# Last self attention: where ScalarE copies the turned weights, between the logarithms of the distances or ahead of them

## The chip, the cores and the metric

The kernel runs on one core of one Trainium2 chip. The metric is device microseconds from start to end of one execution; the kernel before takes 5246.27 us, the median of three runs (5241.81 to 5249.77).

## The reference

The whole is a four-layer stack on x of shape 128 x 32 x 128 (batch, positions, width), each layer a cross attention, a self attention and a feed-forward part with residuals. The change touches the self attention of the last layer alone (16 heads of 8, 32 positions per batch entry), cut here to what it computes:

```python
x = x + _L3_attn_ref(_layernorm(x), Wq, Wk, Wv, Wo)

def _L3_attn_ref(x, Wq, Wk, Wv, Wo):
    q, k, v = (split_heads(x @ W.T) for W in (Wq, Wk, Wv))
    diff_sq = jnp.maximum(q_norm_sq + k_norm_sq - 2.0 * qk, 0.0)
    denom = jnp.maximum((1.0 - q_norm_sq) * (1.0 - k_norm_sq), 1e-06)
    cosh_arg = jnp.maximum(1.0 + 2.0 * diff_sq / denom, 1.0)
    distance = jnp.where(cosh_arg > 1.0, jnp.arccosh(...), 0.0)
    attn = jax.nn.softmax(-distance, axis=-1)
    return (attn @ v, heads joined) @ Wo.T
```

## The kernel before

The 4096 rows of x lie in SBUF as 32 tiles of 128 rows, four batch entries each (TILES = 32, NB = 4). A part of the stack walks over the tiles as a software pipeline. `Plan.run` (L317) unrolls some rounds at either end and puts two rounds into each pass of a hardware loop (step 2) for the rest. In round t an engine works on several tiles at once: `r.third` the layer norm's statistics of t+3, `r.after` the projections of t+2, `r.coming` the scores of t+1, `r.own` the weights of t, `r.turned` the values and the output of t-1. Every engine has its own function `one(r)`, and the order of the calls in it is that engine's order of work: nothing else reorders it. Engines meet in semaphores alone.

The function is `self_attention` with kind "L3" (three self attentions share it). The weights are not computed by an arccosh. ScalarE and VectorE take roots and logarithms in one table set (`natural_log_exp_and_others`, loaded ahead): with D the numerator and E the denominator, root = exp(0.5 ln x), and weights = exp(ln E - 2 ln(sqrt D + sqrt(D+E)) - max).

One round, by engine, in its own order:

- **TensorE** (PE, L1106 on): `middle(t+1)` (L1029, L1031: two pairs of small products into bank MID), `values(t-1)` (L1083 weights times values, L1085 their sums; they read `pT`, the copy of the turned weights), `turn_x(t+2)` (L993), `project(t+2)` (L1006, three products), `scores(t+1)` (L1051, L1053, L1054, L1056, sixteen products), `heads(t-1)` (L1092), `turn(t)` (L1064: the four transposes of the weights into bank T), `output(t-1)` (L1104).
- **ScalarE** (ACT, L1188 on): relu of the distances (L1190: D from PSUM to SBUF), ln of D (L1193; it waits for the relu), exp of half of it (L1195), `take_turned(t-1)` (L1139: copy of bank T into `pT`, and PE's `values` wait for it), ln and exp of D+E (L1200, L1202; the first waits for VectorE's sum L1372), `take_x(t+2)` (L1143: copy that `project` waits for), ln of E (L1206), ln of the root sum (L1208; it waits for VectorE L1384), `take_qkv(t+2)` (L1160), exp of the shifted logarithms (L1214; it waits for VectorE L1391, and `turn(t)` waits for it), `take_heads(t-1)` (L1182: it waits for `heads`, and `output` waits for it).
- **VectorE** (DVE): E = max (L1369), S = D+E (L1372; it waits for the relu), the normalised x of t+2 (L1259), operands of the scores of t+1 (L931 three times), the root sum (L1384; it waits for L1202), the heads over their sums (L1266, L1267, L1278), the logarithms (L1388), their maximum (L1389), the shift (L1391), the squares (L1398), the statistics (L1250 to L1252), the residual (L1286).
- **GpSimd** (POOL): three spreads of the operands (L931), the values by batch entry (L936), the layer norm's root (L947, L949).
- **SyncE** has nothing in this part; it issues no DMA there.

The copy of the turned weights:

```python
def take_turned(t):
    act.wait_ge(turned_written.sem, turned_written.at(t, 1))
    act.wait_ge(pv_done.sem, pv_done.at(t + -1, 1))
    act.activation(s["pT"][:, 0:nt * P], T[:, 0:nt * P], ACT.Copy).then_inc(turned_read.sem, 1)
```

Of the kernel before, what the change touches and what calls it, by code (L numbers as in the profile page):

```python
# [881 lines left out]
def self_attention(k, kind, s):  # L882
# [55 lines left out]
    def heads_first(t):  # L938
        return t.rearrange("p (t b k) -> p b t k", t=4, b=NB)

    def batches_first(t):
        return t.rearrange("p (b t k) -> p b t k", t=4, b=NB)
# [192 lines left out]
    def act(act):  # L1135
# [5 lines that stand above are left out]
        def take_x(t):  # L1141
            act.wait_ge(xT_written.sem, xT_written.at(t, 1))
            act.activation(k.xnT[:, :], A[:, 0:P], ACT.Copy).then_inc(xT_read.sem, 1)  # L1143

        def take_qkv(t):
            act.wait_ge(qkv_written.sem, qkv_written.at(t, 1))
            if kind == "L1":
                act.wait_ge(operands.sem, operands.at(t + -1, 1))
                act.wait_ge(mid_written.sem, mid_written.at(t + -1, 1))
                act.activation(s["qT"], A[:, 0:256], ACT.Copy)  # L1150
                act.activation(s["lat"], A[0:64, 256:384], ACT.Copy).then_inc(qkv_read.sem, 1)
            elif kind == "L2":
                act.wait_ge(mid_written.sem, mid_written.at(t + -2, 1))
                act.wait_ge(ms_ready.sem, ms_ready.at(t + -1, 1))
                act.activation(s["sq"], A[:, 0:160], ACT.Square)
                act.activation(s["qkv"][:, t.odd, :], A[:, 0:192], ACT.Copy).then_inc(qkv_read.sem, 1)
            else:
                act.wait_ge(operands.sem, operands.at(t + -1, 1))
                act.wait_ge(vm_ready.sem, vm_ready.at(t + -1, 1))
                act.activation(s["qkvT"], A[:, 0:3 * P], ACT.Copy).then_inc(qkv_read.sem, 1)  # L1160

        def take_middle(t):
            act.wait_ge(mid_written.sem, mid_written.at(t, 1))
            act.wait_ge(scores_written.sem, scores_written.at(t + -1, 1))
            if kind == "L1":
                act.wait_ge(vm_ready.sem, vm_ready.at(t + -1, 1))
                act.activation(s["kv"], MID[:, :], ACT.Copy).then_inc(mid_read.sem, 1)
            else:
                act.activation(s["qkT"], MID[:, 0:2 * P], ACT.Copy).then_inc(mid_read.sem, 1)

        def take_heads(t):
            if kind == "L1":
                act.wait_ge(pv_done.sem, pv_done.at(t, 1))
                act.wait_ge(out_written.sem, out_written.at(t + -1, 1))
                for j in range(4):
                    d = slice(32 * j, 32 * j + 32)
                    ins = act.activation(s["outT"][d].rearrange("p n (b q) -> p n b q", q=32),
                                         k.psum[d, 3:5, :].rearrange("p n (b c) -> p n b c", c=P)[:, :, :, d], ACT.Copy)
                ins.then_inc(heads_read.sem, 1)
            else:  # L1180
                act.wait_ge(heads_written.sem, heads_written.at(t, 1))
                act.activation(s["outT"][:, 0, :], OUT[:, 0:P], ACT.Copy).then_inc(heads_read.sem, 1)  # L1182

        def one(r):
            if kind != "L3" and r.turned:
                take_turned(r.t + -1)
            if kind == "L3":
                if r.own:  # L1188
                    act.wait_ge(scores_written.sem, scores_written.at(r.t, 1))
                    act.activation(s["D"], D[:, :], ACT.Relu).then_inc(d_ready.sem, 1)  # L1190
                if r.own:
                    act.wait_ge(d_ready.sem, d_ready.at(r.t, 1))
                    act.activation(s["sD"], s["D"], ACT.Ln, bias=s["tiny"]).then_inc(log_step.sem, 1)  # L1193
                    act.wait_ge(log_step.sem, log_step.at(r.t, 1))
                    act.activation(s["sD"], s["sD"], ACT.Exp, scale=0.5)  # L1195
                if r.turned:
                    take_turned(r.t + -1)
                if r.own:
                    act.wait_ge(scores_read.sem, scores_read.at(r.t, 1))
                    act.activation(s["S"], s["S"], ACT.Ln).then_inc(log_step.sem, 1)  # L1200
                    act.wait_ge(log_step.sem, log_step.at(r.t, 2))
                    act.activation(s["S"], s["S"], ACT.Exp, scale=0.5).then_inc(roots.sem, 1)  # L1202
                if r.after:
                    take_x(r.t + 2)
                if r.own:
                    act.activation(s["R"], s["E"], ACT.Ln)  # L1206
                    act.wait_ge(root_sum.sem, root_sum.at(r.t, 1))
                    act.activation(s["S"], s["sD"], ACT.Ln).then_inc(logs_ready.sem, 1)  # L1208
                if r.after:
                    take_qkv(r.t + 2)  # L1210
                if r.own:
                    act.wait_ge(shifted.sem, shifted.at(r.t, 1))
                    act.wait_ge(turned_written.sem, turned_written.at(r.t + -1, 1))
                    act.activation(heads_first(s["pr"]), batches_first(s["R"]), ACT.Exp).then_inc(probs_ready.sem, 1)  # L1214
                if r.turned:
                    take_heads(r.t + -1)
                return
            if kind == "L1":
                if r.coming:
                    take_middle(r.t + 1)  # L1220
                if r.own:
                    act.wait_ge(scores_read.sem, scores_read.at(r.t, 1))
                    act.activation(s["pr"][:, 0:256], s["pr"][:, 0:256], ACT.Exp).then_inc(exp_ready.sem, 1)
            if kind == "L2" and r.own:
                act.wait_ge(scores_written.sem, scores_written.at(r.t, 1))
                act.activation(s["D"], D[:, :], ACT.Tanh, scale=float(1.0 / (CAP * np.sqrt(8.0)))).then_inc(scores_read.sem, 1)
                act.wait_ge(scores_read.sem, scores_read.at(r.t, 1))
                act.wait_ge(probs_ready.sem, probs_ready.at(r.t + -1, 1))
                act.activation(s["E"], s["D"], ACT.Exp, scale=CAP).then_inc(exp_ready.sem, 1)
            if r.after:  # L1230
                take_x(r.t + 2)
                take_qkv(r.t + 2)
            if kind == "L2" and r.coming:
                take_middle(r.t + 1)
            if r.turned:
                take_heads(r.t + -1)

        if kind == "L3":
            act.preload_act_table_set("natural_log_exp_and_others")
            act.wait_ge(set_up.sem, set_up.at(1))  # L1240
        plan.run(act, one)

    def dve(dve):
# [2618 lines left out]
```

## Time and profile before

| what | value |
|---|---|
| median of 3 runs | 5246.27 us (5241.81 to 5249.77) |
| profiled execution, its own time | 5233.18 us |
| span of its instructions | 5231.3 us |
| PE / VectorE / ScalarE / GpSimd busy | 89% / 61% / 41% / 35% |
| mean granted clock of TensorE | 0.937 of full |

The profile is of one execution. Its span runs from the first instruction to the last; about 2 us of the execution's own time lie around it. A line such as L1139 is a line of the kernel, and a helper's line is shared by its callers: L1139 and L931 also serve the other self attentions, so that they are read in the stretch of this part alone (about 4308 to 4699 us). "Idle before, <-releaser" is the time in which the engine did nothing just before an instruction, and what ended it. Times in the timeline are microseconds from the start of the span.

### The profile page before, as it was taken

The numbers are of one execution on the slowest core, as the hardware profiler recorded it, in microseconds if no ns is written. First come the engines' busy times: TensorE is split into PE (matmuls) and PEld (weight loads), VectorE is DVE, ScalarE is ACT, GpSimd is POOL, SyncE is SP. The second block draws the span as 40 slices with busy tenths as digits, with TensorE's granted clock in tenths as the row PEclk, the third lists the DMA queues.
The fourth block names the chain that finished last, engine by engine and source line by source line (L and its number), as shares of the span: only waits on it lengthen the run. The fifth ranks groups of instructions, "written<-read, shape, count | busy, mean of one in ns | idle before, by whom it ended". The sixth has DMA issues, their size and how long they took to land.

```text
span 5231.3 us, 141331 instructions
## 1 busy us (share of the span) xinstructions
PE 4657.2 (89%) x50169; PEld 3698.7 (71%) x50169; DVE 3165.2 (61%) x9513; ACT 2156.9 (41%) x5339; POOL 1845.0 (35%) x2796
## 2 busy tenths in 40 slices
PE   4999999989989999895929999778999989988999
PEld 3777777779957777674717777665577768875776
DVE  3777777756546666555426665775466657764443
ACT  1444444422224444341305555332255545543333
POOL 2555555521013333345043443980044434330000
PEclk8999999999989999996959999898899998888999
DMA  6000000000000100001211110002111100005665
GB/s 203 18 18 17 18 18 18 18 2 2 1 17 29 32 28 28 1 0 32 78 50 34 32 32 25 0 0 72 45 35 32 32 17 0 0 0 121 144 143 133
DMA packets 112438, 199.72 MB, mean 38 GB/s; under 512 B 13315, under 2 KB 54659, under 8 KB 111259
## 3 DMA queue, kind: packets, MB, share of 16 engines
q1 hardware_dynamic: 108147, 188.67, 13.8%
q0 software_dynamic: 4096, 8.40, 0.6%
q8 instruction: 129, 2.11, 0.2%
q14 instruction: 66, 0.54, 0.0%
HBM read 183.29 MB, written 18.97 MB: 39 GB/s over the span
## 4 chain that ended last, share of the span: by engine, by line
PE 75%; DVE 7%; issue 6%; ACT 5%; POOL 4%; SPq 1%; DMA 1%; POOLq 1%; DVEq 0%; ACTq 0%
PE psum_banks L555 6%; PE psum_banks L3089 6%; PE psum_banks L3098 5%; PE psum_banks L560 5%; PE psum_banks L620 4%; PE psum_banks L664 4%; PE psum_banks L671 3%; PE psum_banks L1637 3%; PE psum_banks L624 3%; PE psum_banks L1672 2%; PE psum_banks L2117 2%; PE psum_banks L2784 2%; PE psum_banks L1613 2%; ACT scratch L1755 1%; PE psum_banks L2104 1%
## 5 line engine op out<-in xcount | busy, mean ns | idle before, releaser
L787 DVE TENSOR_REDUCE scratch<-psum_banks 128x2 f32<-128x514 f32 x768 | 531.3, 692 | 409.7 <-PE psum_banks L555 405.6
L706 ACT ACTIVATE scratch<-psum_banks 128x512 f32<-128x512 f32 x768 | 458.7, 597 | 489.3 <-PE psum_banks L565 477.5
L560 PE MATMUL psum_banks<-scratch 32*128 32x128 f32 x6144 | 638.5, 309 | 8.1 <-ACT scratch L706 6.1
L555 PE MATMUL psum_banks<-scratch 32*128 32x257 f32 x3072 | 575.3, 440 | 50.1 <-DVE scratch L788 49.9
L560 PEld LDWEIGHTS psum_banks<-scratch 32*128 32x128 f32 x6144 | 475.7, 185 | 17.3 <-ACT scratch L706 8.6
L555 PEld LDWEIGHTS psum_banks<-scratch 32*128 32x128 f32 x3072 | 254.6, 188 | 272.0 <-issue 175.3
L3098 PEld LDWEIGHTS psum_banks<-w_L_ffn_down,scratch 128*128 128x128 f32 (+1 forms) x2560 | 335.6, 193 | 156.2 <-issue 127.5
L3089 PE MATMUL psum_banks<-scratch,w_L_ffn_up 128*128 128x512 f32 (+1 forms) x752 | 381.9, 603 | 8.2 <-DVE scratch L3276 8.2
L3276 DVE TENSOR_TENSOR scratch<-scratch 128x512 f32<-128x512 f32 x304 | 210.3, 692 | 268.3 <-ACT scratch L3142 234.3
L3142 ACT ACTIVATE scratch<-psum_banks 128x512 f32<-128x512 f32 x320 | 190.8, 597 | 430.2 <-PE psum_banks L3089 430.1
L565 PE MATMUL psum_banks<-shift_T,own_batch 32*128 32x128 bf16 x3072 | 350.8, 214 | 0.0
L3098 PE MATMUL psum_banks<-w_L_ffn_down,scratch 128*128 128x128 f32 (+1 forms) x2560 | 342.5, 277 | 9.1 <-DVE scratch L3276 9.1
L620 PE MATMUL psum_banks<-scratch 128*32 128x128 f32 x6144 | 317.9, 279 | 1.5 <-ACT scratch L706 1.5
L624 PE MATMUL psum_banks<-scratch,consts 128*32 128x128 f32 x6144 | 308.7, 273 | 0.0
L1755 ACT ACTIVATE scratch<-psum_banks,scratch 128x258 f32<-128x258 f32 x512 | 238.4, 473 | 98.4 <-DVE scratch L1840 97.6
L728 ACT ACTIVATE scratch<-psum_banks,c_L_xattn_bk 128x256 f32<-128x256 f32 x384 | 182.4, 475 | 221.1 <-PE psum_banks L671 220.7
L513 POOL TENSOR_TENSOR ln_vareps<-ln_meanvar,ln_eps 128x1 f32<-128x1 f32 x96 | 18.2, 190 | 716.4 <-DVE ln_meanvar L797 716.4
L1534 POOL TENSOR_TENSOR scratch<-scratch 128x512 f32<-128x512 f32 x256 | 269.1, 1051 | 0.0
L1613 PE MATMUL psum_banks<-scratch 128*128 128x257 f32 x1024 | 266.9, 383 | 1.3 <-ACT scratch L1772 0.8
L1637 PE MATMUL psum_banks<-scratch 128*128 128x512 f32 x512 | 247.1, 604 | 11.3 <-ACT scratch L1765 10.5
L1613 PEld LDWEIGHTS psum_banks<-scratch 128*128 128x128 f32 x1024 | 179.7, 190 | 55.4 <-issue 39.8
L936 POOL TENSOR_TENSOR scratch<-scratch,consts 128x512 f32<-128x512 f32 x128 | 140.5, 1107 | 220.4 <-PE psum_banks L1080 131.1
(496 smaller groups left out, 12268.7 us busy)
## 6 DMA issues: line engine op xcount, KB each, us to landing
scratch<-route_T SPq DMA_DIRECT2D x136, 512.0 KB, 7.4
scratch<-in_ctx SPq DMA_DIRECT2D x99, 514.0 KB, 3.5
scratch<-in_ctx_rows SPq DMA_DIRECT2D x130, 128.0 KB, 2.1
scratch<-route_T SPq DMA_DIRECT2D x8, 1024.0 KB, 8.9
expert_rows<-in_ctx SPq DMA_DIRECT2D x10, 512.0 KB, 17.9
scratch<-expert_rows SPq DMA_DIRECT2D x16, 192.0 KB, 2.7
expert_out<-scratch SPq DMA_DIRECT2D x16, 192.0 KB, 2.1
w_L_ffn_up<-in_L_ffn_up SPq DMA_DIRECT2D x1, 2992.0 KB
```

What stands on the lines that cost most here:

```text
L555: return pe.matmul(S[:, g % 2, :], qbd[q, t.odd, (s // 2) * P:(s // 2 + 1) * P], kT_of[q, t.odd, s // 2, :], start=True, stop=True)
L560: return pe.matmul(W[:, g % 2, c * P:(c + 1) * P], kT_of[q, t.odd, b, c * P:(c + 1) * P], qbd[q, t.odd, b * P:(b + 1) * P], start=True, st ...
L565: return pe.matmul(W[:, g % 2, c * P:(c + 1) * P], own_batch[q, b:b + 1].to_broadcast([32, P]), shiftT[q, t.odd, :], start=False, stop=Tru ...
L620: pe.matmul(PV[q, cols], vS[:, t.odd, b, c, q], pT[:, b % 2, g, c, :], start=False, stop=(c == 1), skip_group_check=True)
L624: mm = pe.matmul(SUM[q, cols], k.c("ones")[:, 0:32], pT[:, b % 2, g, c, :], start=False, stop=(c == 1), skip_group_check=True)
L706: act.activation(pT[:, b % 2, 2 * h:2 * h + 2].rearrange("p t c q -> p t (c q)"), W, ACT.Exp).then_inc(exp_ready.sem, 1)
L787: dve.tensor_reduce(parts[:, r.t.odd, 2 * h:2 * h + 2, 0, b], S, X_AXIS, ALU.max, negate=True)
L1613: mm = pe.matmul(S[:, t, 0:KEYS], qa[:, t, b * P:(b + 1) * P], a["zT"][:, b % 2, :], start=True, stop=True, skip_group_check=True)
L1637: mm = pe.matmul(PV[:, :], zk_of[:, b, c, :], a["pT"][:, c, :], start=(c == 0), stop=(c == 1))
L1755: ins = act.activation(a["p"][:, 4 * (b % 2) + t, :], S[:, t, 0:W], ACT.Exp, bias=a["negm"][:, u:u + 1], accum_out=a["rs"][:, u:u + 1])
L3089: mm = pe.matmul(U(u, o)[0:rows(c), :], up_cols(c, o), x, start=True, stop=True)
L3098: mm = pe.matmul(Y[g % 2][:, i * P:(i + 1) * P], a["h"][0:rows(c), u % 3, i * P:(i + 1) * P], down[0:rows(c), c, :], start=(c == 0 and i = ...
```

## The change

In ScalarE's order `take_turned(r.t + -1)` moves from behind the exp of the distances' logarithms (L1195) to between the relu (L1190) and the first logarithm (L1193). Nothing is added or removed, and no other engine's code is touched. The parts ahead of it and behind it, and the other two self attentions, keep theirs.

```diff
@@ -1188,13 +1188,13 @@
                 if r.own:
                     act.wait_ge(scores_written.sem, scores_written.at(r.t, 1))
                     act.activation(s["D"], D[:, :], ACT.Relu).then_inc(d_ready.sem, 1)
+                if r.turned:
+                    take_turned(r.t + -1)
                 if r.own:
                     act.wait_ge(d_ready.sem, d_ready.at(r.t, 1))
                     act.activation(s["sD"], s["D"], ACT.Ln, bias=s["tiny"]).then_inc(log_step.sem, 1)
                     act.wait_ge(log_step.sem, log_step.at(r.t, 1))
                     act.activation(s["sD"], s["sD"], ACT.Exp, scale=0.5)
-                if r.turned:
-                    take_turned(r.t + -1)
                 if r.own:
                     act.wait_ge(scores_read.sem, scores_read.at(r.t, 1))
                     act.activation(s["S"], s["S"], ACT.Ln).then_inc(log_step.sem, 1)
```

## Rows read from the trace of the kernel before

**Rows 1.** The page: busy time of each engine, and PE's granted clock by slice.
```profile
PE 4657.2 (89%) x50169; PEld 3698.7 (71%) x50169; DVE 3165.2 (61%) x9513; ACT 2156.9 (41%) x5339; POOL 1845.0 (35%) x2796
...
PEclk8999999999989999996959999898899998888999
```

**Rows 2.** Stretches (start:end, length, busy, clock, DMA): 28 rounds, single rounds, four rounds.
```profile
4319.55:4664.36 344.81, 321.36 (x2158) 292.49 (x2156) 249.45 (x503) 177.79 (x336) 139.85 (x168) 0.86 0.00 0
4431.90:4442.77 10.87, 10.07 (x81) 9.00 (x78) 8.62 (x18) 6.40 (x13) 4.45 (x7) 1.00 0.00 0
...
4453.49:4465.99 12.50, 11.70 (x81) 10.64 (x78) 9.24 (x18) 6.40 (x13) 6.86 (x9) 0.86 0.00 0
4465.99:4479.71 13.72, 12.86 (x77) 11.82 (x77) 8.84 (x18) 6.31 (x13) 4.64 (x7) 0.75 0.00 0
...
4502.93:4558.10 55.17, 51.87 (x311) 47.44 (x308) 35.27 (x72) 25.41 (x49) 19.24 (x26) 0.75 0.00 0
```

**Rows 3.** Groups by line in 4320 to 4680 us, the idle time before them last.
```profile
L1083 PE MATMUL psum_banks<-scratch 128*128 128x128 f32 x240 | 65.1, 364 | 13.1 <-ACT scratch L1139 13.1
...
L1372 DVE TENSOR_TENSOR scratch<-scratch 128x512 f32<-128x512 f32 x30 | 28.5, 950 | 5.2 <-DVE scratch L1369 3.4
...
L1200 ACT ACTIVATE scratch<-scratch 128x512 f32<-128x512 f32 x30 | 18.9, 631 | 10.8 <-DVE scratch L1372 9.9
...
L1006 PE MATMUL psum_banks<-x_normed_T,w_L_attn_Wq 128*128 128x128 f32 x58 | 18.4, 410 | 10.6 <-ACT x_normed_T L1143 10.6
```

**Rows 4.** Timeline of the round at 4431.90 us, PE and ScalarE.
```profile
4431.52 0.60 PE L1064 MATMUL psum_banks<-consts,scratch 128*128 128x128 f32 x4
...
4431.90 0.59 ACT L1190 ACTIVATE scratch<-psum_banks 128x512 f32<-128x512 f32 x1
...
4432.52 0.72 ACT L1193 ACTIVATE scratch<-scratch 128x512 f32<-128x512 f32 x1
...
4433.28 0.63 ACT L1195 ACTIVATE scratch<-scratch 128x512 f32<-128x512 f32 x1
...
4433.53 0.48 PE L1031 MATMUL psum_banks<-consts 1*128 1x128 f32 x2
...
4433.81 0.58 ACT L1139 ACTIVATE scratch<-psum_banks 128x512 f32<-128x512 f32 x1
...
4434.44 0.49 PE L1083 MATMUL psum_banks<-scratch 128*128 128x128 f32 x2 [0.43 <-ACT scratch L1139]
...
4436.59 0.28 ACT L1143 ACTIVATE x_normed_T<-psum_banks 128x128 f32<-128x128 f32 x1 [0.81 <-PE psum_banks L993]
```

**Rows 5.** Timeline of the round at 4442.77 us: what holds ScalarE before L1143.
```profile
4444.78 1.38 DVE L1372 TENSOR_TENSOR scratch<-scratch 128x512 f32<-128x512 f32 x1 [0.23 <-DVE scratch L1369]
...
4446.86 0.63 ACT L1202 ACTIVATE scratch<-scratch 128x512 f32<-128x512 f32 x1
...
4447.55 0.28 ACT L1143 ACTIVATE x_normed_T<-psum_banks 128x128 f32<-128x128 f32 x1
```

**Rows 6.** Timeline of the round at 4453.49 us, ScalarE and VectorE.
```profile
4458.19 0.28 ACT L1143 ACTIVATE x_normed_T<-psum_banks 128x128 f32<-128x128 f32 x1 [0.35 <-PE psum_banks L993]
```
```profile
4458.01 1.28 DVE L931 TENSOR_TENSOR scratch<-psum_banks,consts 128x512 f32<-128x512 f32 x2
```

**Rows 7.** Timeline of the round at 4465.99 us: PE before the values, ScalarE before L1143.
```profile
4468.62 0.60 PE L1083 MATMUL psum_banks<-scratch 128*128 128x128 f32 x2 [0.42 <-ACT scratch L1139]
...
4472.35 0.28 ACT L1143 ACTIVATE x_normed_T<-psum_banks 128x128 f32<-128x128 f32 x1 [2.33 <-PE psum_banks L993]
```

**Rows 8.** Stretches: the openings of the rounds at 4431.90 and 4466, and their values.
```profile
4431.90:4434.70 2.80, 2.37 (x15) 1.66 (x13) 1.87 (x5) 2.64 (x6) 2.01 (x3) 1.00 0.00 0
4434.40:4436.60 2.20, 2.11 (x17) 1.92 (x17) 2.20 (x6) 1.27 (x3) 0.13 (x1) 1.00 0.00 0
4466.00:4468.80 2.80, 2.31 (x11) 1.57 (x12) 1.78 (x4) 2.50 (x5) 1.83 (x2) 1.00 0.00 0
4468.60:4472.30 3.70, 3.68 (x17) 3.41 (x17) 3.00 (x7) 1.26 (x2) 0.21 (x1) 0.53 0.00 0
```

## The prediction

> **What bounds the kernel now.** I read the page first, then the groups by line, the timeline of single rounds and the stretches of the part that changes. On the page PE is busy for 89% of the span, and it is the only engine near its limit [rows 1]; its clock by slices is near 0.8 where this part runs, the 34th to 36th of 40. In the part, each of the 28 rounds between the relus at 4319.55 and 4664.36 us has PE busy for 321.36 of 344.81 us in all, with VectorE at 249, ScalarE at 178, GpSimd at 140, so PE sets the pace, at a mean granted clock of 0.86 [rows 2]. DMA moves nothing there.
>
> Two things cost PE time. The first is two waits per round. PE stands idle before the values (L1083) until ScalarE's copy L1139 is done, 13.1 us over 30 rounds, 0.44 us each, and before the projections (L1006) for ScalarE's L1143, 10.6 us in all [rows 3]. The second is the clock. There are three kinds of round [rows 2]: 11 of the 28 take 10.6 to 10.9 us, all at a granted clock of 1.00 (2.4 GHz); 6 take about 12.5 us (0.86); 11 take 13.7 to 13.9 us (0.75: half of the round at 1.2 GHz). One row of each kind stands there. Against 10.8 us for a round at full clock the 28 rounds cost 344.8 - 302.4 = 42.4 us more: 11 x 2.95 = 32 from the last kind, 10 from the middle one.
>
> **The change, step by step.** *What moves.* One copy per round, 0.58 us of ScalarE, moves ahead of L1193 and L1195. No instruction is added or removed, no DMA and no other queue is touched.
>
> *Can the copy run there?* It needs the transposes (L1064). They end at 4431.52 + 0.60 = 4432.12, the relu at 4431.90 + 0.59 = 4432.49: they are done 0.37 us earlier. Its second wait (the values of the tile before) ended a round ago. So it starts at about 4432.5 and ends at 4433.1, not at 4434.39 [rows 4].
>
> *What PE gains by it.* PE ends the products before the values at 4433.53 + 0.48 = 4434.01 and starts the values at 4434.44 [rows 4]. The copy will be done 0.9 us before PE is free, so the wait of 0.43 us goes, whole. What is late next is L1143, behind L1202 on ScalarE, and the scores' operands.
>
> *What waits behind the copy.* L1193, L1195, L1200 and L1202 are queued behind it. The first two start one copy (0.5 to 0.6 us) later. Nobody takes their result before L1384, which needs L1202 anyway. From the relu to L1200 ScalarE does the same four instructions, so L1200 is no later. It may be about 0.1 us earlier: L1193 starts 0.62 us after the relu on whose result it waits, while L1139 starts 0.53 us after L1195, which itself takes 0.63 [rows 4]. The Trainium skill, page "ScalarE: Activation LUTs", section "What ACT_TABLE_LOAD costs", says that back-to-back activations overlap by about 93 ns; by it three overlaps instead of two would be worth about 0.1 us a round. The trace bears the size out, but L1200 waited for VectorE's L1372 9.9 us over the 30 rounds [rows 3], so I take nothing for it; the bounds are 0 and 28 x 0.1 = 3 us.
>
> *How much of 0.43 us reaches the end of the round.* PE's next stop is L1143, which needs L993 and a free ScalarE.
> - Rounds like that at 4431.90 (6 of the 28): ScalarE stood 0.81 us idle before L1143 [rows 4]. All passes: 6 x 0.40 = 2.4 us.
> - Rounds like that at 4442.77 (6): VectorE's L1372 takes 1.38 us (its mean is 0.95 [rows 3]), L1202 ends at 4447.49, and L1143 starts at 4447.55 with no idle before it [rows 5]. Nearly nothing passes: 6 x 0.02 = 0.1 us.
> - Rounds like that at 4453.49 (5): L1143 had 0.35 us of slack, but the last operand for the scores is ready only at 4458.01 + 1.28 = 4459.29, and the scores come soon after the projections [rows 6]. I take 0.15: 5 x 0.15 = 0.8 us.
> - Rounds at the low clock (11): ScalarE stood 2.33 us idle there [rows 7]. All passes: 11 x 0.40 = 4.4 us.
>
> Sum: 7.7 us; the bounds are 0 and 28 x 0.43 = 12.
>
> *The clock.* The round at 4465.99 opens as the one at 4431.90 does: PE is busy for 2.31 of its first 2.80 us there, for 2.37 here, both at full clock. Then the clock falls in the one and stays in the other, and the same 17 matmuls of the values take 3.70 instead of 2.20 us [rows 8]. What PE did before it fell was therefore not a long stop: the longest idle in that opening is the wait for L1139, 0.42 us [rows 7]. With so small a difference between an opening that keeps the clock and one that loses it, 0.43 us more of matmuls in the opening, 15% of those 2.80 us, ought to tip many of the 11 rounds. No row shows how many. The bounds are 0 and 11; I take two thirds, 7, since the two openings differ by less than the change adds. The falls inside the scores (the 6 rounds of 12.5 us) follow a stretch from values to projections that is only moved, so I leave them. Seven rounds give back 7 x 2.95 = 20.6 us, and as they then are of the first kinds, they keep only half of their 0.40: minus 1.4.
>
> *Sum:* 7.7 + 20.6 - 1.4 = 26.9, so 27 us less. The profiled execution takes 5233.2 us by its own clock and would take 5206; it ran 13 us under the median of the three runs, 5246.3, from which I count: 5219 us.
>
> **The rivals.**
> *The clock doesn't care* (5238.6 us). Only the wait goes, 7.7 us. For it: the mean clock is set by all that PE does and the change adds no matmul. Against it: rows 8. The Trainium skill, page "TensorE: Matmul & The Clock Gate", section "HAM oscillation — how this bites in real kernels", ties the falling clock to waits that are long beside the bursts of matmuls; by that rule a gap of 0.43 us changes nothing, and the time would be this one. The trace disagrees so far, since the clock falls here behind an opening whose longest idle is 0.42 us [rows 7].
>
> *The wait moves* (5245 us). If VectorE and GpSimd fall behind, all rounds become like that at 4442.77, L1143 or the operands hold PE, and 28 x 0.02 to 0.05, about 1 us, is left. For it: L1372 is slow in some of the rounds at full clock already [rows 3, 5]. Against it: the low-clock rounds, 11 of 28, have 2.3 us to spare.
>
> *Slower* (5262 us). The clock falls in the opening of rounds that now keep it: a shorter round comes to the point of the fall at another phase, and low rounds come in chains (four in a row fill the 55.17 us from 4502.93 on, at 0.75 [rows 2]). One more low round costs 2.95 us, so from the third on (3 x 2.95 > 7.7) the change loses, and from the seventh on by over 0.2%; with 8 of the 11 quick rounds it is 8 x 2.95 - 7.7 = 16 us slower, with all of them 25. Against it: the opening is then denser than any that lost the clock.
>
> *The change doesn't do what it says.* The copy could wait for L1064 behind the relu and hold L1193. The row gives it 0.37 us to spare [rows 4]; I hold this for nearly excluded and give it no chance of its own.
>
> **How the numbers follow.** Forecast (wait gone, part of the clock back) 0.64; clock unchanged 0.16; wait moved 0.09; slower 0.11. About 0.2% (10.5 us) can be told from no change. The forecast's own range is from 3 low rounds (14 us less) to all 11 and the 12 us of direct gain (5246 - 32 - 12, near 5202). For 8 in 10 the range also takes in the second case and the third, to 5245; the slower case and the furthest of the gain (all of the 42 us and more) stay out. Faster by over 0.2%: the forecast and a little of the second case, 0.67. Within 0.2%: the rest of the second, the third and the mildest part of the slower case, 0.25. Slower: 0.08.
>
> **What would show it.** Right: in the groups, L1083's wait for L1139 gone (13.1 us to under 2); L1139 at 0.5 to 0.6 us after the relu; the 28 rounds in 318 us or so at a mean clock of 0.90 to 0.95, with about four rounds of 13.3 us. Clock rival: 337 us, clock still 0.86, the 13.7 us rounds become 13.3. Moved wait: L1006's wait for L1143 grows from 10.6 towards 20 us, or PE shows idle time before L1051. Wrong altogether: more rounds at 0.75 than 11, or a time above 5246.

## The result and the profile after

The changed kernel takes 5217.46 us, the median of five runs (5211.12 to 5223.29), against 5246.27 us (now of five runs, 5241.81 to 5262.64). The medians differ by 28.8 us; the ratio is 0.9941, with a 95% interval of 0.993 to 0.9953, which is about 31 us less. A second set of runs of the same two kernels gave 5196.56 against 5225.51 us, ratio 0.9943 (0.9931 to 0.9955). Of the executions of all kernels one, of the kernel with the copy half way back, was in a slow state (7753 us at a granted clock of 0.547) and is left out of its ratio. The forecast was 5219 us, between 5202 and 5245.

The page of the changed kernel, the line that answers to [rows 1]:

```profile
PE 4631.6 (89%) x50169; PEld 3668.8 (70%) x50169; DVE 3166.8 (61%) x9513; ACT 2151.2 (41%) x5339; POOL 1853.0 (36%) x2796
```

The page alone says little: the same number of instructions on each engine, and 26 us less of busy PE. PE was not given less to do; it did a part of it at the higher clock. The stretches of the changed kernel, 28 rounds between the same two relus and then three of four rounds in a row (columns as in [rows 2]; the last row is the opening of the round at 4484.0):

```profile
4341.09:4650.79 309.70, 294.24 (x2158) 264.37 (x2156) 251.82 (x503) 174.61 (x337) 150.21 (x169) 0.96 0.00 0
4484.01:4495.11 11.10, 10.43 (x81) 9.16 (x78) 9.24 (x18) 6.29 (x14) 5.83 (x7) 1.00 0.00 0
4495.11:4505.75 10.64, 10.05 (x77) 8.99 (x77) 8.92 (x18) 6.19 (x13) 5.03 (x7) 1.00 0.00 0
4505.75:4518.06 12.31, 11.80 (x81) 10.72 (x78) 9.25 (x18) 6.29 (x14) 7.05 (x8) 0.86 0.00 0
...
4484.00:4486.80 2.80, 2.80 (x19) 2.15 (x17) 1.85 (x3) 2.33 (x5) 2.80 (x4) 1.00 0.00 0
```

The part fell from 344.81 to 309.70 us, by 35.1. The reader should look at the clock column: 0.86 became 0.96, with the same 2158 matmuls. The rounds at 0.75 [rows 2] are gone, all 11 of them. Seven rounds between 11.86 and 12.34 us are left; the others run at 1.00. The fourth of the rounds above, right behind the one at 0.86, takes 10.27 us; six rounds stand in that place and take 10.22 to 10.38 us, while no round of the kernel before is under 10.64. The opening of a round, whose first 2.80 us had PE busy for 2.31 to 2.37 before [rows 8], now has no gap.

In the seven rounds the clock falls at the projections, right behind PE's wait for L1143, and is back within the scores, as two stretches of the round at 4505.75 show:

```profile
4505.70:4510.50 4.80, 4.37 (x30) 3.44 (x28) 3.82 (x6) 3.88 (x9) 4.65 (x5) 1.00 0.00 0
4510.50:4514.20 3.70, 3.62 (x17) 3.62 (x18) 3.51 (x8) 1.55 (x4) 0.75 (x1) 0.54 0.00 0
```

The groups in those 28 rounds of the changed kernel, which answer to [rows 3]:

```profile
L1083 PE MATMUL psum_banks<-scratch 128*128 128x128 f32 x224 | 51.2, 318 | 0.0
...
L1051 PE MATMUL psum_banks<-scratch 128*128 128x128 f32 x224 | 48.1, 299 | 2.4 <-DVE scratch L931 1.5
...
L1259 DVE TENSOR_SCALAR x_normed<-x_tokens,ln_meanvar,ln_rstd 128x128 f32 x28 | 25.3, 904 | 0.0
```

The wait for the copy is gone (12.3 us in the same 28 rounds before), and a small new one for VectorE's operands stands ahead of the scores. VectorE's L1259 takes 904 ns on average, from 491, and L1372 takes 988, from 947. One round of the changed kernel at full clock, ScalarE (to set beside [rows 4]; the copy's two lines now stand above, so that L1195 is now the logarithm of D and L1197 its exp), then rows of PE and VectorE:

```profile
4484.01 0.59 ACT L1190 ACTIVATE scratch<-psum_banks 128x512 f32<-128x512 f32 x1
4484.49 0.60 ACT L1139 ACTIVATE scratch<-psum_banks 128x512 f32<-128x512 f32 x1
...
4487.06 0.63 ACT L1200 ACTIVATE scratch<-scratch 128x512 f32<-128x512 f32 x1 [0.70 <-DVE scratch L1372]
...
4488.50 0.28 ACT L1143 ACTIVATE x_normed_T<-psum_banks 128x128 f32<-128x128 f32 x1
```

```profile
4486.06 0.49 PE L1083 MATMUL psum_banks<-scratch 128*128 128x128 f32 x2
...
4488.14 0.32 PE L993 MATMUL psum_banks<-consts,x_normed 128*128 128x128 f32 x1
```

```profile
4485.83 1.20 DVE L1372 TENSOR_TENSOR scratch<-scratch 128x512 f32<-128x512 f32 x1
4486.95 1.06 DVE L1259 TENSOR_SCALAR x_normed<-x_tokens,ln_meanvar,ln_rstd 128x128 f32 x1
```

The copy starts 0.48 us after the relu and ends 1.08 after it, about a microsecond before PE asks for it (L1083 starts at 4486.06).

The profiled execution is only 15.7 us shorter than that of the kernel before, since it reached this part later: the second relu stands at 4341.09 instead of 4319.55 us. In the second profile of the changed kernel it stands at 4327.44, and the 28 rounds take 309.84. So what comes ahead of the part differs by 14 us between the two profiles, and the part itself by 0.1. Much of this goes with the chip: of the kernels below, the four profiled on one chip reach the second relu at 4319.99 to 4322.40 us, the four on another at 4336.40 to 4350.07.

The kernel before was profiled once, and how far its 344.81 us vary from one execution to another isn't on record. Against it all kernels here but one gain 2 to 14 us more in the part than in the median of the whole (35 against 29 for the changed kernel); the one with the late copy loses 83 in the part and 100 in the whole. A difference of a few us between a part and 344.81 us shows nothing by itself. From here on the 28 rounds are compared, and the ratio for the whole.

### The profile page after: what moved, and what is told of

It reads as the page before. It is cut to its first block, busy times and chain, and to the rows that moved or that the text cites. A ratio compares the mean times of both kernels' runs of the same rounds, so it can differ in the third digit from the quotient of the medians.

```text
span 5215.6 us, 141331 instructions
## 1 busy us (share of the span) xinstructions
PE 4631.6 (89%) x50169; PEld 3668.8 (70%) x50169; DVE 3166.8 (61%) x9513; ACT 2151.2 (41%) x5339; POOL 1853.0 (36%) x2796
## 4 chain that ended last, share of the span: by engine, by line
PE 74%; DVE 9%; issue 6%; ACT 4%; POOL 3%; SPq 1%; DMA 1%; another core or an unknown queue 1%; POOLq 1%; DVEq 0%; ACTq 0%
PE psum_banks L555 6%; PE psum_banks L3089 6%; PE psum_banks L3098 5%; PE psum_banks L560 5%; PE psum_banks L620 4%; PE psum_banks L664 4%; PE psum_banks L671 3%; PE psum_banks L1637 3%; PE psum_banks L624 3%; PE psum_banks L1672 2%; PE psum_banks L2117 2%; PE psum_banks L2784 2%; PE psum_banks L1613 2%; ACT scratch L1755 1%; PE psum_banks L2104 1%
## 5 line engine op out<-in xcount | busy, mean ns | idle before, releaser
L521 POOL TENSOR_TENSOR scratch<-scratch,consts 128x512 f32<-128x512 f32 x96 | 100.6, 1048 | 305.9 <-DVE scratch L814 208.3
```

## The experiments

The theory: PE's idle time in the opening of a round is what costs the clock, and the clock is most of the gain. Its rivals: the gain is the 0.43 us of wait itself; or it is ScalarE's order.

**The wait filled, the order of before.** Two products that nobody reads (`fill(bank, n)` issues n times the product of two constants into `bank[:, P:2 * P]`, fp32, 128 columns), in PE's wait ahead of the values:

```diff
         def values(t):
+            if kind == "L3":
+                pe.wait_ge(heads_ready.sem, heads_ready.at(t + -1, 1))
+                fill(SUM, 2)
             pe.wait_ge(turned_read.sem, turned_read.at(t, 1))
```

> The kernel before with its order kept, and two products nobody reads (fp32, 128 columns, into free columns of the sums' bank, about 0.22 us each) in PE's wait ahead of the values: the copy is as late as before, only PE is busy while it waits. If the gain comes mostly from the clock (my theory), the values still start about 2.6 us after the relu, but the rounds of 13.7 us go: 28 rounds in 310 to 325 us instead of 344.8, mean clock 0.92 to 0.97, the execution 15 to 30 us under before. If only the wait counts (rival), nothing is gained: 28 rounds in 343 to 350 us, clock 0.86, time as before within 5 us.

Measured: ratio 0.9938 (0.9925 to 0.9951), 28 rounds in 304.74 us. The stretch, and PE and ScalarE in one round of it (in this kernel L1198 is the relu, L1147 the copy, L997 the two added products, L1091 the values):

```profile
4321.75:4626.49 304.74, 293.41 (x2270) 265.25 (x2268) 255.25 (x503) 177.70 (x336) 145.90 (x168) 1.00 0.00 0
```

```profile
4411.00 0.71 PE L997 MATMUL psum_banks<-consts 128*128 128x128 f32 x4
4411.55 0.39 PE L1091 MATMUL psum_banks<-scratch 128*128 128x128 f32 x2
```

```profile
4408.87 0.60 ACT L1198 ACTIVATE scratch<-psum_banks 128x512 f32<-128x512 f32 x1
...
4410.79 0.58 ACT L1147 ACTIVATE scratch<-psum_banks 128x512 f32<-128x512 f32 x1
```

The copy is as late as before (1.92 us after the relu), and the values begin 2.68 us after it, no earlier than the 2.54 of [rows 4]. PE does 112 matmuls more in the 28 rounds (each product shows as two). Yet every round is at full clock and the part is 40 us shorter. In the part this is more than the whole gain of the change, and the values begin no earlier.

**Half of the wait filled** (`fill(SUM, 1)` in the same place).

> The kernel before with one product instead of two in PE's wait ahead of the values: half of the wait is filled. The clock answers to each product by steps: more rounds of 10.7 to 11.1 us than before, but some at 0.75 or 0.86 are left, 28 rounds between 305 (two products) and 344.8 us (none); my value is 318, the execution 15 to 28 us under before. The rival (no effect of the filling, the two products of the other run did something else, such as moving the phase once) gives 343 to 346 us.

Measured: ratio 0.9957 (0.9944 to 0.997), 28 rounds in 312.57 us at 0.97; two rounds of 13.65 and two of 12.5 us are left. The effect comes in steps with the filling: 344.8, 312.6, 304.7 us for none, one and two products. In the part the first product does most of it, more than I had thought (318); by the ratios of the whole it does some 70% (0.43 of 0.62%).

**The copy early, the values held back.** In the changed kernel L1195's exp (now L1197) gives a signal of its own, and the values wait for it:

```diff
-                    act.activation(s["sD"], s["sD"], ACT.Exp, scale=0.5)
+                    act.activation(s["sD"], s["sD"], ACT.Exp, scale=0.5).then_inc(half_root.sem, 1)
...
+            if kind == "L3" and r.turned and r.own:
+                pe.wait_ge(half_root.sem, half_root.at(r.t, 1))
             if r.turned:
                 values(r.t + -1)
```

> The changed kernel, its copy early, but PE's values are held back by a semaphore until ScalarE's L1195 of the round is done (about 2.4 us after the relu; before the change the values began at 2.63, after it at 2.13). Nothing is computed in the hold. If PE's idle time in the opening is what lowers the clock (my theory), most of the gain goes again: rounds at a granted clock of 0.75 come back, 28 rounds in 325 to 345 us, the execution 0 to 20 us under before. If the early copy itself is what pays (a shorter path on ScalarE), the gain stays: 28 rounds in 307 to 313 us.

Measured: ratio 0.9995 (0.9986 to 1.0003): the execution has lost the gain. The 28 rounds and the values' group of this kernel:

```profile
4350.07:4687.85 337.78, 315.30 (x2158) 286.30 (x2156) 252.20 (x503) 174.85 (x337) 140.12 (x168) 0.88 0.00 0
```

```profile
L1084 PE MATMUL psum_banks<-scratch 128*128 128x128 f32 x224 | 58.5, 354 | 11.0 <-ACT scratch L1200 11.0
```

In this kernel L1084 is the first product of the values and L1200 the exp that gives the signal. PE idles 11.0 us in 28 openings (0.39 each), and rounds of 13.7 us are back (seven from 13.72 to 13.86, one of 15.4). The part is still 7 us under the one profile of before, which the whole doesn't show. ScalarE has the changed order here, so that order in itself is worth nothing that can be told from zero.

**The copy half way back**, between L1193 and L1195's exp.

```diff
                     act.activation(s["sD"], s["D"], ACT.Ln, bias=s["tiny"]).then_inc(log_step.sem, 1)
+                if r.turned:
+                    take_turned(r.t + -1)
+                if r.own:
                     act.wait_ge(log_step.sem, log_step.at(r.t, 1))
```

> The copy between the first logarithm (L1193) and its exp (L1195), half way back. It ends about 1.8 us after the relu, and PE is free for the values at 2.05 to 2.15. If what counts is that the copy is done before PE asks for it, this is as fast as the changed kernel (28 rounds in 305 to 315 us, ratio 0.994). If the earliest possible copy counts, or the overlap of ScalarE's instructions, it lies between the two kernels (5225 to 5235 us).

Measured: ratio 0.9942 (0.993 to 0.9955), 28 rounds in 309.81 us: the same as the changed kernel to 0.1 us. What counts is that the copy is done when PE asks; earlier than that bought nothing here.

**The copy one step later**, behind L1200.

```diff
-                if r.turned:
-                    take_turned(r.t + -1)
                 if r.own:
                     act.wait_ge(scores_read.sem, scores_read.at(r.t, 1))
                     act.activation(s["S"], s["S"], ACT.Ln).then_inc(log_step.sem, 1)
+                if r.turned:
+                    take_turned(r.t + -1)
```

> The copy one step later than before, behind the logarithm of D+E (L1200): PE's wait ahead of the values grows from 0.43 to about 1.1 us or more. Wait alone: 28 x 0.65 = 18 us more in rounds that PE sets, so 5255 to 5265 us. With the clock: the opening is sparser still, more rounds run at 0.75, 28 rounds in 370 to 395 us, and the execution takes 5270 to 5295 us. If the wait was hidden, no change from before.

Measured: ratio 1.0199 (1.0186 to 1.0212), 100 us over before, beyond every value I gave.

```profile
4320.83:4749.05 428.22, 368.86 (x2158) 339.05 (x2156) 248.03 (x503) 174.51 (x336) 136.11 (x169) 0.75 0.00 0
```

```profile
L1083 PE MATMUL psum_banks<-scratch 128*128 128x128 f32 x224 | 76.4, 441 | 48.2 <-ACT scratch L1139 48.2
```

The wait grew to 48.2 us, 1.7 a round, since the copy now also stands behind L1200's own wait for VectorE's L1372, which I had counted as nothing (0.59 us in the round at 4395.71). That is 36 us more of waiting than before, and the part is 83 us longer; PE's busy time went up by 47.5 us for the same matmuls. The clock's share is again the larger. From the third round on four lengths (about 16.1, 16.7, 15.1 and 13.6 us) come by turns, at clocks from 0.68 to 0.87.

**PE's other wait filled.** The changed kernel with two unread products ahead of the projections:

```diff
+            if kind == "L3" and r.after and r.turned:
+                fill(T, 2)
             if r.after:
                 project(r.t + 2)
```

> The changed kernel plus two products nobody reads (0.22 us each, into the bank of the turned weights, which is free then) in PE's second wait, ahead of the projections (L1006, 0.37 us a round). By the clock theory the remaining rounds of 12.2 us, whose clock falls in the scores, go or get fewer: 28 rounds in 297 to 305 us instead of 309.7, clock near 1.00, 5 to 12 us under the changed kernel. If the clock doesn't care about such a gap: 309 to 315 us, no gain, or up to 3 us lost where the products outlast the wait.

Measured: ratio 0.9947 (0.9934 to 0.996), 28 rounds in 305.20 us at 0.98. Of the seven rounds over 11.8 us one is left (12.13), and two of 11.66. The part gained 4.5 us on the changed kernel, just short of what I expected: as neighbouring rounds at full clock took 11.11 and 10.64 us by turns, there was nothing under 10.9 on average to be had. The ratio of the whole doesn't tell it from that of the changed kernel. With this wait filled three rounds with a fall are left of seven, so most of these falls too seem to hang on idle time of PE, that ahead of the projections. One of the two rounds of 11.66 us lost the clock without a stop, though: PE was busy for 11.60 us of it.

**Is the 0.43 us slack at full clock?** The changed kernel with two unread products ahead of the values, where there is no wait to fill:

> The changed kernel with two unread products ahead of the values, where PE has no wait now: PE gets 0.45 us more work in every round. If the 0.43 us that the change gives PE are slack at full clock (what the runs so far suggest), all rounds stay at full clock, 28 rounds take 304 to 306 us, as with the wait filled in the kernel before, and it is 3 to 6 us faster than the changed kernel although it does more. If PE's own work sets the round at full clock, 28 x 0.3 to 0.45 us are added: 313 to 318 us.

> The changed kernel once more, for a comparison on the same chip with the two beside it: ratio 0.994 to before, 28 rounds in 309 to 311 us, clock 0.96, whatever the parts ahead of it do; the start of the part may differ by some 20 us between executions, in both kernels alike.

Measured on one chip: 5191.88 us with the extra work (ratio 0.9932, 0.9919 to 0.9945), 5196.56 without it. The 28 rounds of the first:

```profile
4326.70:4631.41 304.71, 292.97 (x2270) 264.45 (x2268) 255.24 (x503) 174.71 (x336) 146.04 (x168) 1.00 0.00 0
```

The part is 5.1 us shorter than the 309.84 of the changed kernel beside it, although PE does more. The kernel with the late copy and the same two products took 304.74. These two don't weigh the 0.43 us, though: the products fill the time that the early copy frees, and in both kernels the values begin 2.68 us after the relu. What weighs it is the changed kernel's own rounds. There the values begin 2.05 us after the relu, and two neighbouring rounds at full clock take 11.10 and 10.64 us; here, with the values 0.63 us later, they take 11.11 and 10.67 to 10.72. So in a row of rounds at full clock the early values bring 0.02 to 0.05 us a round. Only in the six rounds right behind a fall (10.22 to 10.38 us) does more of it seem to pass; no run separates how much.

**GpSimd's spread earlier.** In the changed kernel the first of its three L931 goes ahead of the layer norm's root, which then is that of t+2 in the next round:

```diff
                     rows_by_head(pool, s["kbd"][:, 1, :], s["sq"][:, P:2 * P], k.c("quad"))
+                if r.after:
+                    normal(r.t + 2)
+                if r.coming:
                     rows_by_head(pool, s["kbd"][:, 0, :], s["qkvT"][:, P:2 * P], k.c("quad"))
...
-            if kind != "L2" and r.third:
+            if kind == "L1" and r.third:
                 normal(r.t + 3)
```

> The changed kernel, and GpSimd issues the first of its three spreads ahead of the layer norm's root instead of behind it, so that the spreads end some 1 to 1.4 us earlier in the round and share less time with VectorE's L1372 and L1259. If the operands and L1372 are what took the direct gain (the rounds of 11.10 us at full clock), L1372 is at 0.7 to 0.75 us in nearly all rounds, these rounds fall to 10.7, and 28 rounds take 295 to 305 us. If PE alone sets the full-clock round, 309 us stay. Rival against both: L1259 waits for the later root, 2 to 6 us lost.

> The last two ideas together: GpSimd's first spread early, and two unread products in PE's wait ahead of the projections. Full clock in nearly all rounds and no slow L1372: 28 rounds in 290 to 298 us (10.3 to 10.6 a round), 8 to 15 us under the changed kernel. If the shorter rounds meet the clock's fall again, 300 to 310 us.

> GpSimd's first spread early and two unread products ahead of the projections, on the same chip as the changed kernel: 28 rounds in 299 us at a clock of 1.00, 8 to 12 us under the changed kernel, ratio to before 0.992.

Alone it brings nothing: ratio 0.9949 (0.9937 to 0.9962), 28 rounds in 309.34 us. The rounds at full clock did fall, from 11.10 and 10.64 us to 10.73 and 10.57, but about every fourth still takes 12.0 to 12.2, and L1372 did not get faster (mean 1237 ns, from 988): I was wrong on the means. L1259 did (559 ns, from 904). Together with the products ahead of the projections the clock stays:

```profile
4336.40:4635.48 299.08, 291.91 (x2270) 264.48 (x2268) 248.61 (x503) 173.34 (x336) 142.21 (x169) 1.00 0.00 0
```

Ratio 0.9931 (0.9918 to 0.9943), and on another chip 0.993 (0.9917 to 0.9943), 5189.99 us beside the 5196.56 of the changed kernel; the part took 301.64 us there, with one round of 13.29. The 299.08 us are just above the 290 to 298 that I had expected, the 301.64 above the 299. It is the fastest seen in this part; in the whole the intervals of its ratio and of the changed kernel's overlap, and its lead of 6.6 us is under the 8 to 12 expected, though only one of its five runs lies within the range of the changed kernel's six.

## Why the prediction was right, and which of its terms were not

- *The wait goes, whole*: as forecast. The copy is done 1 us before PE asks, and L1083's idle time is 0.0 us in 28 rounds, from 12.3.
- *Nobody misses what waits behind the copy*: as forecast; the roots' L1202 ends at 4488.35 us, before L1143 is due (4488.50). The 0.1 us of overlap shows (L1139 starts 0.48 us after the relu, where L1193 started 0.62 after it) and is worth nothing, as L1200 still waits for VectorE's L1372 (0.70 us in the round at 4484).
- *The direct gain, 7.7 us*: mis-sized; in a row of rounds at full clock it measures 0.02 to 0.05 us a round, and with the six rounds right behind a fall it is some 0.5 to 4 us in all (an estimate: 28 x 0.02 us at least; at most 22 x 0.05, and six times 0.5 us, from 10.22 to 10.38 us against 10.64 and more in other rounds). I had read how much of the 0.43 us each kind of round would pass on from the rounds as they were. But the rounds to which nearly all of it passed were those at the low clock and those right behind one, and the low ones vanished. At full clock it stops at VectorE: in the round at 4484 L1372 takes 1.20 us (0.74 in the round at 4431.90) and L1259 1.06 (0.34), so that the normalised x is ready at 4488.01 and L993 starts at 4488.14, and L1051 waits 0.17 us for the operands. That was the rival "the wait moves", and for this term it was right: its second sign, idle time of PE before L1051, is there (2.4 us in 28 rounds from 0.0), while L1006's wait, the first sign, stayed at 10.3 us.
- *The clock, 20.6 us less 1.4*: mis-sized the other way. I gave back 7 of the 11 low rounds; all 11 went. The two thirds were a guess between two bounds, as no row showed how many. With a clock of 1.00 and two products more a round the part takes 304.7 us, so the clock had 40 us to give, and the change gained 35. The rounds of the middle kind stayed, as forecast (7 now, 6 before), but the prediction misread where their clock falls: not inside the scores but at the projections, behind PE's wait for L1143 (in the round at 4453.49 the first two products of L1006 take 0.74 us, where they take 0.49 in the round at 4431.90). That wait stayed, and with it filled three of the seven rounds are left.
- *The sum*: 318 us for the 28 rounds against 309.7 measured, 27 us less in the whole against 29 to 31. By that the direct term was 4 to 7 us too high, and the clock's 12 to 15 too low. That 5219 lies within 2 us of the measured median is luck in good part: the two errors offset each other, and the whole gained some 5 us less than the part. One bound doesn't follow from its terms either: 3 low rounds with the direct gain make 16 us (3 x 2.95 + 7.7 - 0.6), not 14.
- *The rival "the clock doesn't care"* falls: filling the wait without removing it moved the clock from 0.86 to 1.00, and holding PE back took it from 0.96 to 0.88. The Trainium skill, page "TensorE: Matmul & The Clock Gate", section "HAM oscillation — how this bites in real kernels", speaks of waits long beside the bursts of matmuls. No such wait is in this part (the longest in the opening of [rows 7] is 0.42 us), and the clock answered to it all the same, once a round.
- *Slower*: not seen with the forecast order. That the clock can fall in more rounds is shown by the copy one step later (0.75 on average, 428.2 us), but there PE waits longer; the rival's own mechanism, a shorter round that meets the fall at another phase, no run shows.

Not settled: why the part ahead differs between chips and executions, how far the part of the kernel before varies, and what precisely decides whether a round loses the clock. Idle time in a round isn't all of it. With two products ahead of the values no round lost the clock, although the wait ahead of the projections stayed whole (10.3 us in 28 rounds); and the round of 13.29 us above lost it, although PE was busy for 13.22 us of it and for 10.64 of the 10.74 us of the round before it.

## What to carry to other kernels

Where PE sets the pace and its granted clock is under full, look at its short idle gaps before its work: make the producer of the first late operand finish before PE asks, and price a gap by the rounds that lose the clock and not by its own length. Whether the clock is the cause can be tested cheaply, by filling the gap with products that nobody reads; if the kernel gets faster by doing more, and the granted clock rises, it is. And where the forecast is a sum over kinds of rounds, ask which of the kinds will still exist.

## What I had not expected of the hardware

Two unread products in every round, 0.55 us of PE's time from the start of the first to the start of the values (4411.00 to 4411.55 us), made the execution 0.62% faster (ratio 0.9938), although PE had 112 matmuls more to do in the 28 rounds; one product alone made it 0.43% faster. And the wait of 1.7 us a round, 36 us more in all, cost 83 us in the part. VectorE's L1259 took 491 ns on average before and 904 in the changed kernel, though nothing in its own code had changed.
